# A decoder layer on one core: the prologue's projections in other PSUM banks, K's rotation in its own buffer, and q 1 and q 2 taken earlier

## The reference, cut to what matters

```
x = x + attention(layernorm(x))          # 32 heads of 64, 8 groups of keys and values, rotary, causal
x = x + ssm(ctx, z=layernorm(x), ...)    # selective scan over the context, gated by silu(z)
x = x + ffn(layernorm(x))                # quantised, 256 -> 704 -> 256

# attention
q, k = apply_rope(q), apply_rope(k)      # x * cos + rotate_half(x) * sin
attn = softmax(causal(q @ k.T * scale))
out  = (attn @ v) @ Wo.T
# ssm, the part that is done in the prologue
xi = in_proj_w @ ctx                     # 256 channels
u  = silu(conv1d(xi, 4 taps) + conv_b)
x_dbl = x_proj_w @ u                     # 40 rows: dt_lo, B, C
delta = softplus(dt_proj_w @ dt_lo + dt_proj_b)
```

## Time and profile before

| | |
|---|---|
| median of 3 runs | 438.95 us (438.73 to 439.83) |
| profiled execution | 438.5 us, span 436.7 us |
| PE busy | 385.6 us, 88% of the span |
| DVE busy | 347.2 us, 80% |
| ACT busy | 268.8 us, 62% |
| POOL busy | 181.8 us, 42% |
| chain that ended last | PE 39%, DVE 18%, issue 17%, DMA 11% |

### The profile page before, as it was taken

One profiled execution on the slowest core, in us unless ns is written; L12 is line 12 of the kernel. 1 busy time (PEld: TensorE's weight loads), 2 busy tenths in 40 slices (PEclk: granted clock), 3 DMA queues, 4 the chain that ended last, 5 costly groups with the idle time before them and its releaser, 6 DMA issues.

```text
span 436.7 us, 7777 instructions
## 1 busy us (share of the span) xinstructions
PE 385.6 (88%) x2636; PEld 307.6 (70%) x2636; DVE 347.2 (80%) x479; ACT 268.8 (62%) x775; POOL 181.8 (42%) x262
## 2 busy tenths in 40 slices
PE   4879988999999988998899899988875999699996
PEld 2546776877887767786778677766664887488885
DVE  1766757888898998899989988998988998476532
ACT  2465799666776667666766666766653677543221
POOL 2653442355546254625562546354642453120000
PEclk9989999999999999999999999999999899889999
DMA  9852265358865679397656682965566942200000
GB/s 229 162 107 53 62 146 169 107 175 176 210 152 152 119 165 222 95 230 184 138 159 133 158 220 64 228 143 138 162 133 161 205 102 53 50 0 26 25 26 24
DMA packets 55431, 57.42 MB, mean 131 GB/s; under 512 B 32984, under 2 KB 43424, under 8 KB 55392
## 3 DMA queue, kind: packets, MB, share of 16 engines
q0 software_dynamic: 9792, 22.10, 25.1%
q1 hardware_dynamic: 35712, 28.44, 24.7%
q10 hardware_dynamic: 9888, 6.39, 5.1%
HBM read 26.36 MB, written 1.18 MB: 63 GB/s over the span
## 4 chain that ended last, share of the span: by engine, by line
PE 39%; DVE 18%; issue 17%; DMA 11%; ACT 6%; POOL 6%; SPq 2%; DVEq 0%; ACTq 0%; POOLq 0%
PE ps_p L1086 8%; DMA y<-state 6%; PE ps_so L1103 6%; PE ps_p L1313 5%; PE ps_so L1296 5%; PE ps_r L1155 4%; DVE nmax L745 4%; DVE state L825 4%; ACT prob L481 3%; POOL rc L403 3%; PE ps_p L1203 3%; DMA qt<-rc 2%; DMA bc<-bc_scratch 2%; DVE state L838 2%; PE ps_so L1114 2%
## 5 line engine op out<-in xcount | busy, mean ns | idle before, releaser
L481 ACT ACTIVATE prob<-ps_so,nmax 128x256 f32<-128x256 f32 (+1 forms) x256 | 104.7, 441 | 51.8 <-DVE nmax L745 51.7
L403 POOL TENSOR_TENSOR rc<-rc,rs 128x512 f32<-128x512 f32 x40 | 58.4, 1460 | 105.0 <-DVE rs L733 66.7
L832 DVE TENSOR_TENSOR_SCAN state<-decay,state 128x1024 f32<-128x1024 f32 x32 | 73.3, 2292 | 1.1
L487 ACT ACTIVATE pt<-ps_r 128x512 f32<-128x512 f32 x96 | 53.7, 593 | 31.6 <-PE ps_r L1155 31.6
L1086 PE MATMUL ps_p<-xt_all,wq 128*128 128x256 f32 x256 | 63.8, 392 | 9.9 <-DVE rs L737 4.9
L273 POOL DMA_DIRECT2D qt<-rc x128 | 65.0, 520 | 10.0 <-POOL rc L403 9.5
L745 DVE TENSOR_REDUCE nmax<-ps_so 128x2 f32<-128x512 f32 (+1 forms) x96 | 60.2, 683 | 10.5 <-PE ps_so L1114 10.5
L1086 PEld LDWEIGHTS ps_p<-xt_all,wq 128*128 128x128 f32 x256 | 46.2, 190 | 23.3 <-DVE rs L737 6.6
L1203 PE MATMUL ps_p<-wo,attn_t 128*128 128x256 f32 x256 | 60.9, 383 | 0.2 <-DVE attn_t L848 0.2
L410 POOL DMA_DIRECT2D y<-state x32 | 29.8, 932 | 73.1 <-DVE state L838 70.9
L481 ACT ACTIVATION_READ_ACCUMULATOR prob<-ps_so,nmax 128x1 f32 x256 | 57.9, 226 | 0.0
(11 more groups left out here) (108 smaller groups left out, 524.9 us busy)
## 6 DMA issues: line engine op xcount, KB each, us to landing
bc<-bc_scratch SPq DMA_DIRECT2D x32, 512.0 KB, 5.2
y<-state POOLq DMA_DIRECT2D x32, 512.0 KB, 5.9
qt<-rc SPq DMA_DIRECT2D x128, 32.0 KB, 2.4
qt<-rc POOLq DMA_DIRECT2D x128, 32.0 KB, 2.2
wo<-wo_t ACTq DMA_DIRECT2D x8, 256.0 KB, 4.3
wq<-wqkv_t SPq DMA_DIRECT2D x28, 64.0 KB, 2.5
kt<-kt SPq DMA_DIRECT2D x7, 256.0 KB, 3.0
kt<-rc POOLq DMA_DIRECT2D x34, 32.0 KB, 1.8
```

Source lines behind the costliest of these rows:

```text
L403: nc.gpsimd.tensor_tensor(rc[:, r % 2, :, :], rc[:, r % 2, :, :], rs[:], ALU.add).then_inc(rope_add, 1)
L481: nc.scalar.activation(o, i, ACT.Exp, bias=nmax[:, r, c:c + 1], accum_out=rsum[:, r, GRP + head:GRP + head + 1]).then_inc(exp_done, 1)
L487: nc.scalar.activation(pt[:, fill, :], ps_r[:, fill % 2, :], ACT.Copy).then_inc(pt_copied, 1)
L832: nc.vector.tensor_tensor_scan(state[:, v % 2, :], decay[:, v % 2, :], state[:, v % 2, :], 0.0, ALU.mult, ALU.add).then_inc(decay_free, 1)
```

## The change

It touches the prologue alone; the units' code is the same but for three waits of unit 0.

- Context projection 0 goes to banks 2 and 3 of `ps_so`, context projection 1 to the two banks of `ps_r`, the first half of xdbl to bank 3 of `ps_so`. Scores 0 wait for convolution 0 alone; convolution 1 is waited for by the first transposes of the probabilities, and the copies of xdbl by values 0.
- K 0's rotation is made in the two buffers of `rep_s` (which unit 0 uses only later) instead of `rc` and `rs`. q 0's rotation then doesn't wait for K's addition, nor q 1's for K's transfers. The first copy into `rep_s` waits for them instead.
- VectorE rotates q 1 ahead of convolution 1.
- TensorE projects q 2 ahead of scores 0.
- ScalarE issues the second pair of the first key's transfers (GpSimd before) and q 0's head 1 (SyncE before); SyncE issues the loads of wq 3 (ScalarE before).

```diff
+        k_raw = rep_s[:, 0, :].rearrange("p (c s) -> p c s", c=2)
+        k_sin = rep_s[:, 1, :].rearrange("p (c s) -> p c s", c=2)
+        ctx_ps = [ps_so[:, 2:4, :], ps_r[:, :, :]]
+        xdbl_at = [ps_so[0:XR, 3, :], ps_p[0:XR, 1, :]]
...
# SyncE
             move_first_k(sp, 0)
-            move_q(sp, 0, range(GRP // 2), q_sp)
+            move_q(sp, 0, (0,), q_sp)
             move_k(sp, 0, range(1, KG // 2), k_sp)
+            load_wq(sp, 3)
             load_wq(sp, 4)
# GpSimd
             add_rope(("k", 0))
-            move_first_k(nc.gpsimd, 1)
             add_rope(("q", 0))
# ScalarE, in copy_rep
+                if u == 0:
+                    act.wait_ge(k_first[0], 16 * 2)
+                    act.wait_ge(k_first[1], 16 * 2)
+                    act.wait_ge(k_sp[0], k_sp_due(0))
+                    act.wait_ge(k_pool[0], 16 * k_moves)
...
+            move_first_k(nc.scalar, 1)
             first_tap(1)
-            load_wq(nc.scalar, 3)
+            move_q(nc.scalar, 0, (1,), q_sp)
             silu_u(0)
# VectorE, in rope
-                if r >= 2:
+                if r >= 3:
...
-                if r >= 1:
+                if r >= 2:
                     dve.wait_ge(rope_add, r)
+                to, sines = (k_raw, k_sin) if r == 0 else (rc[:, r % 2, :, :], rs[:])
...
             convolve(0, range(2, DC))
+            rope(("q", 1))
             convolve(1, range(1, DC))
-            rope(("q", 1))
             negmax(0)
# TensorE, in project_ctx, fill, scores, transpose_p, values
+                if e:
+                    pe.wait_ge(xt_sb, 1)
...
-                if f == ("q", 2):
-                    pe.wait_ge(xdbl_sb, 2)
...
                 if u == 0:
-                    pe.wait_ge(conv_done, EB * (DC - 1))
+                    pe.wait_ge(conv_done, DC - 1)
...
+                    else:
+                        pe.wait_ge(conv_done, EB * (DC - 1))
...
+                else:
+                    pe.wait_ge(xdbl_sb, 2)
...
             fill(("v", 0))
+            fill(("q", 2))
             scores(0)
 
             pe.wait_ge(ssm_in, 32)
             pe.wait_ge(u_done, EB)
-            pe.wait_ge(rope_mul, 6)
             pe.wait_ge(v_copied, 1)
...
-                    nc.tensor.matmul(ps_p[0:XR, h, :], xproj[:, e, :], u_s[:, e, h * 512:(h + 1) * 512],
+                    nc.tensor.matmul(xdbl_at[h], xproj[:, e, :], u_s[:, e, h * 512:(h + 1) * 512],
...
-            fill(("q", 2))
```

More of the change, by code:

```diff
@@ L279, in move_first_k @@
             for to in (0, HD):
-                queue.dma_start(kt[to + c * HALF:to + (c + 1) * HALF, 0, 0, :], rc[0:HALF, 0, c, :]
+                queue.dma_start(kt[to + c * HALF:to + (c + 1) * HALF, 0, 0, :], k_raw[0:HALF, c, :]
                                 ).then_inc(k_first[c], 16)
@@ L294, in move_k @@
                 for c in range(2):
-                    queue.dma_start(kt[c * HALF:(c + 1) * HALF, j % 2, i, :],
-                                    rc[i * HALF:(i + 1) * HALF, r % 2, c, :]).then_inc(landed[j % 2], 16)
+                    src = rc[i * HALF:(i + 1) * HALF, r % 2, c, :] if j else k_raw[i * HALF:(i + 1) * HALF, c, :]
+                    queue.dma_start(kt[c * HALF:(c + 1) * HALF, j % 2, i, :], src).then_inc(landed[j % 2], 16)
         block = ctx.enter_context(nc.Block())
@@ L402, in add_rope @@
                 pool.wait_ge(rope_mul, 2 * (r + 1))
-                nc.gpsimd.tensor_tensor(rc[:, r % 2, :, :], rc[:, r % 2, :, :], rs[:], ALU.add).then_inc(rope_add, 1)
+                o, s = (k_raw, k_sin) if r == 0 else (rc[:, r % 2, :, :], rs[:])
+                nc.gpsimd.tensor_tensor(o, o, s, ALU.add).then_inc(rope_add, 1)
             def add_y(v):
@@ L560, in first_tap @@
                 act.wait_ge(inp_ps, 2 * e + 2)
-                nc.scalar.activation(du[:, e, :].rearrange("p (h n) -> p h n", h=2), ps_so[:, 2 * e:2 * e + 2, :],
+                nc.scalar.activation(du[:, e, :].rearrange("p (h n) -> p h n", h=2), ctx_ps[e],
                                      ACT.Identity, bias=par[:, e, DC:DC + 1], scale=par[:, e, DC - 1:DC]
@@ L592, in _ @@
                 act.wait_ge(xdbl_ps, i + 1)
-                nc.scalar.activation(xdbl[:, i * 512:(i + 1) * 512], ps_p[0:XR, i, :], ACT.Copy
+                nc.scalar.activation(xdbl[:, i * 512:(i + 1) * 512], xdbl_at[i], ACT.Copy
                                      ).then_inc(xdbl_sb, 1)
@@ L723, in rope @@
                     else:
-                        if i == 0:
-                            dve.wait_ge(k_first[0], 16 * 2)
-                            dve.wait_ge(k_first[1], 16 * 2)
                         dve.wait_ge(k_sp[i % 2], k_sp_due(i))
                         dve.wait_ge(k_pool[i % 2], 16 * k_moves * (i // 2 + 1))
-                if r >= 1:
+                if r >= 2:
                     dve.wait_ge(rope_add, r)
+                to, sines = (k_raw, k_sin) if r == 0 else (rc[:, r % 2, :, :], rs[:])
                 if f[0] == "q":
@@ L734, in rope @@
                 else:
-                    nc.vector.scalar_tensor_tensor(rc[:, r % 2, :, :], ps, HD ** 0.5, cos_s[:], ALU.mult, ALU.mult
+                    nc.vector.scalar_tensor_tensor(to, ps, HD ** 0.5, cos_s[:], ALU.mult, ALU.mult
                                                    ).then_inc(rope_mul, 1)
-                    nc.vector.scalar_tensor_tensor(rs[:], ps[:, ::-1, :], HD ** 0.5, sin_s[:], ALU.mult, ALU.mult
+                    nc.vector.scalar_tensor_tensor(sines, ps[:, ::-1, :], HD ** 0.5, sin_s[:], ALU.mult, ALU.mult
                                                    ).then_inc(rope_mul, 1)
@@ L760, in convolve @@
                 acc = du[:, e, :].rearrange("p (b s) -> p b s", b=B)
-                src = ps_so[:, 2 * e:2 * e + 2, :].rearrange("p h (b s) -> p (h b) s", b=B // 2)
+                src = ctx_ps[e][:, :, :].rearrange("p h (b s) -> p (h b) s", b=B // 2)
                 for lag in lags:
@@ L1042, in project_ctx @@
                 pe.wait_ge(ctx_in, 32)
+                if e:
+                    pe.wait_ge(xt_sb, 1)
                 for h in halves:
-                    nc.tensor.matmul(ps_so[:, 2 * e + h, :], inproj[:, e * P:(e + 1) * P],
+                    nc.tensor.matmul(ctx_ps[e][:, h, :], inproj[:, e * P:(e + 1) * P],
                                      ctxs[:, h * 512:(h + 1) * 512], start=True, stop=True).then_inc(inp_ps, 1)
@@ L1229, in _ @@
                 for e in range(EB):
-                    last = nc.tensor.matmul(ps_p[0:XR, h, :], xproj[:, e, :], u_s[:, e, h * 512:(h + 1) * 512],
+                    last = nc.tensor.matmul(xdbl_at[h], xproj[:, e, :], u_s[:, e, h * 512:(h + 1) * 512],
                                             start=(e == 0), stop=(e == EB - 1))
                 last.then_inc(xdbl_ps, 1)
-            fill(("q", 2))
             def unit(u):
```

## The result

The changed kernel takes 434.81 us in the median of 4 executions (434.68 to 436.37), the kernel before 439.21 of 4; the ratio is 0.9912, with a 95% interval of 0.9891 to 0.9933. It was timed twice more later, beside experiments: 435.53 against 438.59 (0.9930, 0.9903 to 0.9956) and 434.82 against 438.23 (0.9931, 0.9908 to 0.9954). So it is faster by 3.1 to 4.4 us; the forecast was 3.5 us faster, at 435.4.

What follows compares the result with a forecast made beforehand. Bound: a chain on VectorE, then TensorE from 23.55 us. VectorE's 2.72 us plus 0.90 of slack less 0.1 make 3.5; 438.5 becomes 435.0, and 0.45 for the median gives 435.4; range 434.3 to 437.4 for 8 in 10.

Steps and rivals of the forecast that it cites:

- The path through the prologue: Prologue, scores 0 to second dt product: the product begins at 34.1 instead of 37.62, 3.5 us earlier.
- The 0.1 us for the signal and the engine's start: Second dt product behind the first dt addition: some 0.1 us taken off the gain.
- the last of q 1's transfers: SyncE's queue ahead of scores 1: last issued at 27.3, landed at 29.7, needed at 31.5.
- From there to the end: All units behind the prologue: the whole rest moves by 3.5 us, giving 435.0 for the profiled execution.
- the same 3.5 us at each later unit: Sign of being right, in the later units: each shows the prologue's 3.5 us shift.
- (c): Later units: transfers meet others and longer landings give back 3.5 us or leave 1.5; 438.9 if all is lost; 10%.
- (d): Later units: two added waits of 3.5 us as engines take another phase, giving 442.4; 7%.
- (e): Later units: a long landing in the present chain falls away, up to 3.5 us more, 432 to 434.5; 8%.
- rival (a): Scores 0: the clock stays low or they come that much late, gain only 2.4 us, 436.5; 8%.
- since TensorE now works from 6 to 24 us without such a hole, I take the full clock: Scores 0 on TensorE: full clock, so 2.05 us with masks instead of 3.64.
- q 1's rotation ahead of convolution 1: VectorE: 1.28 us moved ahead of the convolution, 0.84 saved from the wait, so convolution ends 0.45 us later.
- Rival (b): ScalarE behind silu 1: the table switch costs up to 1.53 us more, gain 2.4 us, 436.5; 4%.

Runs made afterwards that it cites:

- a1: The changed kernel timed again with no edit, in more rounds: 435.53 us, 0.9903 to 0.9956 of the kernel before.
- d2: The changed kernel again with no edit, beside another experiment on the same chip: 434.82 us, 0.9908 to 0.9954 of the kernel before.
- a2: The kernel before with 28 filler transposes in TensorE's hole ahead of scores 0: 436.56 us, 0.9944 to 1.0007 of the kernel before.
- c1: The kernel before with only K's rotation in its own buffer: 436.90 us, 0.9947 to 0.9985 of the kernel before.
- b1: The changed kernel with q 2's projection behind the xproj products again: 434.60 us, 0.9887 to 0.9947 of the kernel before.
- b2: The changed kernel with q 2's projection and q 1's rotation both back where they were: 434.11 us, 0.9875 to 0.9933 of the kernel before.
- c2: The kernel before with only the new context banks and scores 0 waiting for convolution 0 alone: 438.87 us, 0.9979 to 1.0031 of the kernel before.
- a4: The changed kernel with the issue of transfers as before: 436.10 us, 0.9926 to 0.9984 of the kernel before.

## Why the prediction was right, point by point

**The path through the prologue.** In executions without a fall of the clock it is right to 0.2 us at every point of the path. a1 begins 0.05 us ahead of the kernel before and has scores 0 at 21.88 (forecast 21.95), the first maximum at 23.71 (23.87), the first exponential at 26.11 (26.23), the transposes at 29.50 (29.5), the dt product at 30.52 (30.5), scores 1 at 31.57 (31.55), the second dt product at 33.98 (34.1). The sum was 3.5 us; the shift is 3.55. The 0.1 us for the signal and the engine's start was an estimate without a row; a1 has 0.14 (the dt addition ends at 33.84). Two slips cost nothing: xproj from 24.94 for 3.62 us ends at 28.56, not 28.65, and SyncE issues the last of q 1's transfers at 28.5, not 27.3, with 1.8 us to landing; scores 1, at 31.57, don't wait for them.

**From there to the end.** The shift is handed on without loss through the early units. The reciprocals of units 9 and 31 in the kernel before, and in a1:

```profile
123.98 0.18 DVE L754 RECIPROCAL rinv<-rsum 128x8 f32<-128x8 f32 x1
```

```profile
370.50 0.18 DVE L754 RECIPROCAL rinv<-rsum 128x8 f32<-128x8 f32 x1
```

```profile
120.38 0.18 DVE L764 RECIPROCAL rinv<-rsum 128x8 f32<-128x8 f32 x1
```

```profile
364.17 0.17 DVE L764 RECIPROCAL rinv<-rsum 128x8 f32<-128x8 f32 x1
```

At unit 9 it is 3.60 us, 3.55 counted from the first step. In all other profiles too the shift stays within 0.03 us from unit 1 to unit 9. At unit 31 it is 6.3 us here, 4.4 in d2 and 2.8 in the first profile of the changed kernel, counted from the first step. Nothing of the change lies in between: the later units scatter by 2 us and more from one execution to another. So the sign "the same 3.5 us at each later unit" holds for the early units and not for single executions at the end. The rivals (c), (d) and (e) gave such a scatter to the change; it is there, but in kernels without most of the change too (a2's shift goes from 1.17 to 3.5, c1's from 2.05 to 3.05), and the medians, 3.1 to 4.4 us apart, don't show that the change moves it. That the forecast's 3.5 us is met at the end is so for the medians only. What makes the scatter was not tested.

**The clock, rival (a).** The step "since TensorE now works from 6 to 24 us without such a hole, I take the full clock" held for scores 0 in all three profiles of the changed kernel. The reason given was not what made it so: in b1 and b2 TensorE stood still for 1.46 and 1.43 us ahead of scores 0, in c1 and c2 for 2.6 us and more, and the clock was full there too. Rival (a) priced a low clock in scores 0 at 1.1 us (2.4 instead of 3.5), and a2 gives 1.17. What the forecast lacked was the same fall at another place: it fell in scores 1 in one profile of three, for 1.28 us. That this execution took 436.37, near rival (a)'s 436.5, is luck as to the place.

**The single edits.** The forecast costed them as one path and did not say which could be left out. By the shifts, each kernel against its neighbour: the clock 1.17 (a2); K's buffer 0.88 beside it (c1 less a2); banks, xdbl and transfers 1.60 beyond this (b2 less c1); q 1's rotation ahead -0.68 (b1 less b2; -0.47 counted from q 0's rotation); q 2's projection ahead +0.58 (a1 less b1; +0.37). That these add up to 3.55 is no proof, as each difference begins where the one before ended; and in another order the shares would differ, since the clock alone and the banks alone win the same 1.06 us of waiting (a2, c2). Taking the transfers out of the whole costs 0.9 (a4); what the banks are worth beside the buffer, without the transfers, was not run. The step "q 1's rotation ahead of convolution 1" was costed as 1.28 moved ahead of the convolution, and rightly; what was missing is a sum for the other order, in which ScalarE's silu and exponentials start 1.19 us sooner (b2) and leave room for q 2's projection where it was.

**Rival (b), the switch of tables.** Refuted: the exponential at 26.53 follows the load that ends at 26.51. The drain that the Trainium skill gives in "ScalarE: Activation LUTs", section "What ACT_TABLE_LOAD costs", is not seen in this trace as a gap behind the load, nor ahead of it (24.16 + 1.06 = 25.22, load at 25.23).

## What to carry to other kernels

Here the gain in a prologue could be added up from the timeline to 0.1 us, with each engine's queue followed to the point where two of them meet, as long as the clock did what was assumed; the forecasts of the buffer and the banks alone, in which the clock was not counted, were off by 0.5 us and more. In the loop behind it such a shift was handed on unchanged for nine units, and scatter hid it at the end of single executions, so compare the place of instructions, counted from a common early one, and check with a second one that nothing ahead of the edit has moved. Reorderings should be tested one by one: here two of them cancelled, and the clock, the buffer, the banks and the issue of transfers did the work. When a chain has moved, look at what is on it now: the 2 us of normalising that could be moved stood in plain sight in the new chain.

## What the runs showed that was not expected

TensorE's clock fell to half behind the 3.43 us without work in the kernel before, not behind 2.60 us (c1) or 2.75 us (c2), and yet once behind two gaps of 0.9 and 1.0 us (the first profile of the changed kernel, at about 32.4 us) and once behind waits of 1.15 us and less (a4, at about 37 us), while the same gaps did nothing in a1 and d2. So neither the length of the wait just ahead nor the kernel alone decides it in these runs, and what does was not found. What it costs depends on what hangs on the products: 1.17 us in scores 0, 1.28 us in scores 1, 1.48 us behind the second dt product.
